# Cross-attention with residual and layer norm on one core: values' products ahead of the scores in full slots, loads ahead of slot 0, the last shifts on ScalarE

## The reference

```python
Q = (x @ w_q.T).reshape(B, S, 16, 32).transpose(0, 2, 1, 3)
K = (ctx @ w_k.T).reshape(B, -1, 16, 32).transpose(0, 2, 1, 3)
V = (ctx @ w_v.T).reshape(B, -1, 16, 32).transpose(0, 2, 1, 3)
attn = softmax(einsum('bhqd,bhkd->bhqk', Q, K) / sqrt(32))
c = einsum('bhqk,bhkd->bhqd', attn, V)     # back to (B, S, 512)
z = c @ w_o.T + b_o + x
out = (z - mean(z)) * rsqrt(var(z) + 1e-5) * gamma + beta
```

## Time and profile before

| what | us |
| --- | --- |
| median of 3 runs | 559.24 (558.02 to 559.49) |
| the profiled execution | 559.06 |
| its span, first to last instruction | 557.3 |
| PE busy | 533.4 (96%), 4522 products |
| DVE busy | 465.2 (83%) |
| POOL busy | 424.5 (76%) |
| ACT busy | 393.8 (71%) |
| mean granted TensorE clock | 0.992 |

### The profile page before, as it was taken

How to read it: one execution, slowest core, us unless ns; L and a number is a source line. 1 busy time by engine, 2 the same in 40 slices (tenths; PEclk the granted TensorE clock), 3 DMA queues, 4 the chain that set the end, 5 groups by cost and what they waited for, 6 DMA issues and landing times.

```text
span 557.3 us, 12699 instructions
## 1 busy us (share of the span) xinstructions
PE 533.4 (96%) x4522; PEld 365.2 (66%) x4522; DVE 465.2 (83%) x874; ACT 393.8 (71%) x733; POOL 424.5 (76%) x391
## 2 busy tenths in 40 slices
PE   8988889999999999999999999999999999998991
PEld 6755556766676666766676667666676667665561
DVE  7867658888888888988889888988888888988785
ACT  7636667777777777777777777777777777766662
POOL 1714778888888888888888888888888888776665
PEclk9999999999999999999999999999999999999996
DMA  8434552443344334442343334443343432322122
GB/s 303 150 86 132 147 162 70 131 129 95 95 130 131 102 91 125 130 123 84 113 133 109 120 95 125 107 123 100 120 121 98 133 103 84 85 67 72 44 76 95
DMA packets 74111, 63.23 MB, mean 113 GB/s; under 512 B 46528, under 2 KB 46528, under 8 KB 74048
## 3 DMA queue, kind: packets, MB, share of 16 engines
q1 hardware_dynamic: 74048, 62.42, 37.5%
HBM read 39.58 MB, written 16.78 MB: 101 GB/s over the span
## 4 chain that ended last, share of the span: by engine, by line
PE 81%; DVE 6%; DMA 4%; SPq 3%; issue 2%; POOL 2%; ACT 1%; DVEq 0%; POOLq 0%
PE ps_q L408 28%; PE ps_o L414 27%; PE ps_c L370 9%; PE ps_s L343 7%; DMA max_rows<-max_turned 4%; PE ps_s L353 3%; PE ps_q L281 2%; SPq L215 2%; PE ps_s L281 2%; PE ps_o L281 2%; DVE half_max L701 1%; DVE turned L696 1%; POOL y L877 1%; PE ps_c L288 1%; POOL y L875 1%
## 5 line engine op out<-in xcount | busy, mean ns | idle before, releaser
L408 PE MATMUL ps_q<-x_hi,wq_lo 64*128 64x512 f32 x448 | 186.8, 417 | 1.7 <-DVE values L666 1.6
L414 PE MATMUL ps_o<-wo_hi,c_lo 64*128 64x512 f32 x448 | 186.7, 417 | 0.0
L408 PE MATMUL ps_q<-x_hi,wq_hi 64*128 64x512 f32 x448 | 175.7, 392 | 0.0
L408 PE MATMUL ps_q<-x_lo,wq_hi 64*128 64x512 f32 x448 | 175.5, 392 | 0.0
L414 PE MATMUL ps_o<-wo_hi,c_hi 64*128 64x512 f32 x448 | 175.2, 391 | 0.0
L414 PE MATMUL ps_o<-wo_lo,c_hi 64*128 64x512 f32 x448 | 174.8, 390 | 0.0
L408 PEld LDWEIGHTS ps_q<-x_hi,wq_lo 64*128 64x128 f32 x448 | 82.4, 184 | 70.9 <-DVE z L745 45.3
L875 POOL TENSOR_TENSOR y<-y,gamma_row 128x512 f32<-128x512 f32 x60 | 77.6, 1294 | 58.9 <-ACT y L560 58.9
L847 POOL TENSOR_TENSOR x_lo<-xT_raw,x_hi 128x512 fp32r<-128x512 f32 x60 | 77.6, 1293 | 27.4 <-ACT x_hi L495 25.3
L853 POOL TENSOR_TENSOR c_lo<-c_raw,c_hi 128x512 fp32r<-128x512 f32 x64 | 82.7, 1292 | 17.3 <-ACT c_hi L495 17.2
L414 PEld LDWEIGHTS ps_o<-wo_hi,c_hi 64*128 64x128 f32 x448 | 82.6, 184 | 10.6
(11 more groups left out here) (104 smaller groups left out, 1114.5 us busy)
## 6 DMA issues: line engine op xcount, KB each, us to landing
xT_raw<-in_xT SPq DMA_DIRECT2D x64, 256.0 KB, 3.3
x_raw<-in_x SPq DMA_DIRECT2D x64, 256.0 KB, 2.9
out<-y SPq DMA_DIRECT2D x64, 256.0 KB, 2.4
max_rows<-max_turned SPq DMA_DIRECT2D x256, 16.0 KB
ctx_raw<-in_ctxT SPq DMA_DIRECT2D x4, 256.0 KB, 4.5
wk_raw<-in_wkT SPq DMA_DIRECT2D x4, 256.0 KB, 4.7
wq_raw<-in_wqT SPq DMA_DIRECT2D x4, 256.0 KB, 5.9
wv_raw<-in_wvT SPq DMA_DIRECT2D x4, 256.0 KB, 6.9
```

What stands on the lines that cost most here:

```text
L408: return nc.tensor.matmul(ps_q[:, 0, :], w[l][half, k, dims], x_[r][half, qc % 2, k, :], start=(half is lower and k == 0 and step == 0), s ...
L414: return nc.tensor.matmul(ps_o[:, 0, :], cx[l][half, k, tile], wo[r][half, k, :], start=(half is upper and k == 0 and step == 0), stop=(ha ...
```

## The change

- In the full slots `combine_values(t - 2)` comes ahead of `score(t)`.
- SP issues `wo_raw` (8 DMAs), the bias, gamma, beta and tiles 0 to 3 of `x_raw` ahead of its wait for the keys and of the first fill; slots 2 to 5 load one tile of `x_raw` each.
- In slots 1 to 3 `subtract_max(t - 1)` comes ahead of `project_values`. In slot 6 DVE makes `odd_values` ahead of `turn_max`.
- In slot 62 DVE makes `turn_max(61)` ahead of `divide(59)` and `statistics(54)`.
- The shifts of tiles 59, 60 and 61 are made by ScalarE as two operations on one column each: minus the mean, then times rstd.
- `WARM` is 8.
- `eps_column` (4 bytes in each partition) and the small statistics are allocated behind the streamed tensors.

```diff
@@
-    WARM = 10
+    WARM = 8
@@
-        eps_column = sb("eps_column", [P, 1], fp32)
 
         xT_raw = sb("xT_raw", [P, KT, CHUNK], fp32)
@@
+        half_max = sb("half_max", [P, 2, 32], fp32)
+
+        max_hl, max_turned = sb("max_hl", [P, 3, 32], fp32r), sb("max_turned", [P, 2, 32], fp32)
+        stats = sb("stats", [P, 8, 6], fp32)
+        mean_var = sb("mean_var", [P, 8, 2], fp32)
+        log_var, rstd, shift = (sb(n, [P, 8], fp32) for n in ("log_var", "rstd", "shift"))
+        eps_column = sb("eps_column", [P, 1], fp32)
@@ SP
-            sp.wait_ge(keys_zeroed, 2)
-            sp.wait_ge(keys_lo_done, G)
@@ SP
+            for k in range(KT):
+
+                for head in range(2):
+                    sp.dma_start(wo_raw[64 * head:64 * (head + 1), k, :],
+                                 woT_v[k, :, :].rearrange("(p h d) n -> h p d n", p=2, h=2)[head, :, :, :]
+                                 ).then_inc(wo_loaded[k], 16)
+            sp.dma_start(bias_row[:, :], b_o.partition_broadcast(P)).then_inc(bias_loaded, 16)
+            for row, src in ((gamma_row, gamma), (beta_row, beta)):
+                sp.dma_start(row[:, :], src.partition_broadcast(P)).then_inc(gains_loaded, 16)
+            for i in range(4):
+                load_x(i)
+            sp.wait_ge(keys_zeroed, 2)
+            sp.wait_ge(keys_lo_done, G)
             for t in range(OUT_LAG):
                 fill_max_rows(t)
                 load_ahead(t)
...
                 if 2 <= t <= 5:
-                    load_x(2 * t - 4)
-                    load_x(2 * t - 3)
...
+                    load_x(t + 2)
                 next_keys(t)
@@ PE, head
                 project_queries(t + 1)
+                if 1 <= t <= 3:
+                    subtract_max(t - 1)
...
-                if 1 <= t < OUT_LAG - 1:
+                if 3 < t < OUT_LAG - 1:
                     subtract_max(t - 1)
@@ PE, full slots
                 project_both(t + 1, t - OUT_LAG, True)
+                combine_values(t - 2)
                 score(t)
-                combine_values(t - 2)
@@ ACT
+            def shift_mean(i):
+                c = i % 8
+                nc.scalar.activation(shift[:, c:c + 1], mean_var[:, c, 0:1], ACT.Identity, scale=-1.0
+                                     ).then_inc(mean_negated_done, 1)
+                act.wait_ge(mean_negated_done, by_scalar(i) - by_scalar(59) + 1)
+                act.wait_ge(rstd_done, i + 1)
+                nc.scalar.activation(shift[:, c:c + 1], shift[:, c:c + 1], ACT.Identity, scale=rstd[:, c:c + 1]
+                                     ).then_inc(shift_done, 1)
@@ ACT, end
-            invert_deviation(59)
-            normalise(59)
...
+            for i in (59, 60, 61):
+                invert_deviation(i)
+                shift_mean(i)
+                normalise(i)
@@ DVE, head
+                if t == OUT_LAG - 1:
+
+                    odd_values(t // 2)
                 turn_max(t)
-                if t % 2 == 0:
+                if t % 2 == 0 and t < OUT_LAG - 1:
                     odd_values(t // 2)
@@ DVE, slot 62
+            turn_scores(61)
+            half_maxima(61)
+            fold_halves(61)
+            turn_max(61)
+            divide(59)
+            statistics(54)
+            add_residual(55)
+            queries_to_lo(63)
@@ POOL, end
             for i in (59, 60, 61):
-                shift_mean(i)
                 scale(i)
```

More of the change, by code:

```diff
@@ L78, in cross_attention_kernel @@
         turned = sb("turned", [P, 2 * CHUNK], fp32)
-        half_max = sb("half_max", [P, 2, 32], fp32)
-        max_hl, max_turned = sb("max_hl", [P, 3, 32], fp32r), sb("max_turned", [P, 2, 32], fp32)
         max_rows = sb("max_rows", [P, 2, CHUNK], fp32r)
@@ L89, in cross_attention_kernel @@
         x_raw = sb("x_raw", [P, 8, DM], fp32)
-        stats = sb("stats", [P, 8, 6], fp32)
-        mean_var = sb("mean_var", [P, 8, 2], fp32)
-        log_var, rstd, shift = (sb(n, [P, 8], fp32) for n in ("log_var", "rstd", "shift"))
         with ExitStack() as raw:
@@ L154, in cross_attention_kernel @@
         last_scaled_done, last_y_done = sem("last_scaled_done"), sem("last_y_done")
+        mean_negated_done = sem("mean_negated_done")
         def key_blocks(t, s, j):
@@ L242, in _ @@
                 load_ahead(t)
[L244 to L251, removed]
-                if 2 <= t <= 5:
-                    load_x(2 * t - 4)
-                    load_x(2 * t - 3)
-                if t == 5:
-                    for row, src in ((gamma_row, gamma), (beta_row, beta)):
-                        sp.dma_start(row[:, :], src.partition_broadcast(P)).then_inc(gains_loaded, 16)
+                if 2 <= t <= 5:
+                    load_x(t + 2)
                 next_keys(t)
@@ L772, in _ @@
                 queries_to_lo(t + 1)
+                if t == OUT_LAG - 1:
+                    odd_values(t // 2)
                 turn_max(t)
-                if t % 2 == 0:
+                if t % 2 == 0 and t < OUT_LAG - 1:
                     odd_values(t // 2)
-            for t in range(OUT_LAG, SLOTS - 1):
+            for t in range(OUT_LAG, SLOTS - 2):
                 i = t - OUT_LAG
```

## The result

| | us |
| --- | --- |
| before | 559.51 (558.02 to 560.62, 6 runs) |
| after | 573.05 (571.05 to 573.76, 6 runs) |
| ratio | 1.0236 [1.0214, 1.0259] |
| the profiled execution after, its span | 573.76, 571.8 |
| PE, DVE, ACT, POOL busy | 535.9, 470.7, 398.9, 423.8 |

A forecast was written before the change was run, and what follows sets the result against it. PE, with products back to back in the full slots, was taken to bound the kernel, leaving head and tail: head +16.0, full slots +2.1 and 0, tail -1.1 and -2.7, sum +14.3 on 559.06, giving 573.4 us; range 566 to 580.

The forecast's parts named there:

- First fill: Head: wo_raw's eight DMAs queue on two engines, 6.0 us a pair; subtract_max(0) waits until 51.4, +19.2 us.
- The lower end: Head, first fill: at 2.57 us per wo_raw DMA, the fill lands at 47.9 instead of 51.4.
- the share of 0.13: Head, sign of being right: DMA share near 0.13, two engines working, from some 24 to 46 us.
- Clock: Head: after 20 us idle PE returns at 1.2 GHz, 4 us at half speed, +2.0 us (0 to 4).
- rival (4): Head: clock stays full and wo_raw pairs run at 51 GB/s, 568 us; chance 0.12 together with (3).
- Rest of the head: From subtract_max(0) to the first full slot: fills land on time, 36.2 us instead of 41.4, -5.2 us.
- Full slots: The 56 full slots: 0.63 us less cover makes late fills of max_rows cost +2.1 us; PE's step changes by 0.
- Several new waits for `max_rows`: Full slots: listed among the signs that would show the forecast wrong; no size given.
- PE-neutral swap: Full slots: combine_values ahead of score keeps both PE transitions, 2.17 us against 2.16, taken as 0.
- Rivals (2) and (3): Full slots: (2) one more open load, 579 us, chance 0.10; (3) one transition saved, 567.8, 0.12 together with (4).
- Tail: Tail: earlier turn_max(61) brings PE's rows forward, -1.1 us; shifts on ScalarE bring z(63) forward, -2.7 us.
- Rival (1): Head: wo_raw's DMAs spread over other engines, early loads hidden, first fill at 31.6, 551.8 us; chance 0.09.

The follow-up runs named there:

- e1: The changed kernel with the eight wo_raw loads back behind the fills, in slots 1 to 4: 553.9 us, ratio 0.9891 against the kernel before.
- e2: The changed kernel with wo_raw still early but loaded by 16 DMAs of 32 partitions that use all engines: 560.1 us, ratio 1.0007 against the kernel before.
- e14: The changed kernel with 80 added products keeping PE busy ahead of subtract_max(0): 571.5 us, ratio 1.0202 against the kernel before.
- e3: The kernel before with only combine_values moved ahead of score in the full slots: 563.8 us against 559.8, ratio 1.0071.
- e11: e1 with the swap undone, score again ahead of combine_values: 551.4 us, ratio 0.9845 against the kernel before.
- e5: The kernel before with only turn_max(61) moved ahead of divide(59) and statistics(54): 558.7 us, ratio 0.9974.
- e13: As e2, with the bias moved to slot 1 and gamma and beta to slot 5: 556.2 us, ratio 0.9932 against the kernel before.
- e10: The changed kernel with only four of the eight wo_raw loads early, the others in slots 3 and 4: 565.4 us, ratio 1.0094 against the kernel before.
- e4: The kernel before with only the shifts of tiles 59 to 61 moved to ScalarE: 558.8 us, ratio 0.9971.
- e8: The kernel before with only eps_column and the small statistics allocated behind the streamed tensors: 558.7 us, ratio 0.9981.

## Why the prediction was right, step by step

The forecast of the total is better than its terms. Against the trace, the first fill is 2.1 us under the forecast, the rest of the head 1.1 over it and the tail 1.2 over it; that these nearly cancel is luck. What is shown is the mechanism of each term:

- **First fill, +19.2 forecast, +17.1 seen.** The mechanism was right: two engines, always the same, in order, 51 GB/s; e1 (the loads put back) removes the delay whole, e2 (more engines) two thirds of it. The mis-sized term is the pair of `wo_raw`, 6.0 us from the earlier trace rows: eight DMAs took 22.0 us from 21.9 on, 5.5 a pair. The pairs of before had fills and loads of `xT_raw` among them, of which I took off only 0.4. The lower end (2.57 each, 20.6) is what the first three steps show (2.5 to 2.6), until other loads ran beside them; with those it was too low by 1.4. The seven loads (4.6) and the fill (0.7) came as written. That bias, gamma and beta in a row move at 145 to 164 GB/s on all engines (e2, e1), and that the two engines are slower while loads run on the fourteen, I had not seen. For the same reason the share of 0.13, my sign for all of 24 to 46, held only until 32.
- **The Trainium skill's rule** ("DMA: Bandwidth & Descriptors", section "Why a DMA increments its semaphore by 16 and not by 1") spoke against the change, and e2 bears it out: with 32 as the slowest dimension the same bytes land by 28.0, with 2 by 43.8.
- **Clock, +2.0.** e14 gives 2.1. The granted clock was 0.50 from 34 on, in the wait, and until 54, some 5 us after PE began again. So rival (4), a clock that stays full, is out.
- **Rest of the head, -5.2 forecast.** -2.1 seen less 2.1 for the clock is -4.2. Of the missing 1.0, 0.2 is ahead of `score(3)` (e14's 8.94 at full clock, instead of 8.75) and 0.8 is slot 6: 7.33 us instead of 6.55. The fills did land on time: 4.0 to 4.5 us from `max_turned` to the rows in place in slots 1 to 6, where before they took up to 8.2. The combination waits 0.30 for c_raw of divide(3), and the first full slot 0.61 for `odd_values` (88.62 above). I had costed the moved `odd_values` at 0.15 of DVE time and not asked when it is asked for.
- **Full slots, +2.1 and 0.** In after the sum is exact, by two errors that cancel: the longer slots add 4.0 instead of 1.0 us, so +3.0 (forecast 2.1), and the step is 7.828 instead of 7.844, -0.9 (forecast 0). The wait is the one forecast: 0.5 us of cover are left of 1.2, and fills that land 0.6 to 2.0 us late now stop PE. But I took their number, three or four, from before. With the swap there are more: five to eight that take over 4.6 us in each of the eight traces with it, two to five in the six without, many of them 14 slots apart. In after, two of the five waits are for such new ones (fills 29 and 45). Why the swap makes more of them is open. Several new waits for `max_rows` also stood among my signs of being wrong; five came, and they are what this term is made of, so that sign was badly chosen. e3 and the e1/e11 pair give 4.0 and 2.6 for the whole swap, the tail included.
- **PE-neutral swap.** Right: 1.02, 0.34, 0.23, 0.23 as forecast, and the same plain slot in e3. Rivals (2) and (3), an open load more or a transition less for 5.6 us, are out: either would show as 0.1 us in the plain slot, and the largest difference, between e1 and e11, is 0.01.
- **Tail, -3.8 forecast, -2.6 seen.** The shifts gave their 2.7 at z(63), and finish(63) took 0.7 back beside POOL. I had written that POOL slows finish(62), and not that finish(63) comes under it once it is early. turn_max(61) moved PE's rows by 1.3 but the last product only by 0.6: the chain behind it, to `subtract_max(63)`, is late next (e5).
- **Rival (1)** (hidden loads) needed a landing before 37. e2 shows the turning point well: landing at 36.0, time equal to before.

## What to carry to other kernels

Before a load is put ahead of a small, urgent DMA in the same queue, read how many engines it uses and what a packet of it costs: what counts is not the bytes but the time of the busiest engine, here 22 us for 1 MB. A swap that is neutral on the bounding engine still spends somebody's cover; list the transfers whose cover it takes, and their slowest landings rather than the typical one, and allow for more slow ones than before. In a tail, ask of each operation that is brought forward what it will then run beside.

## What the runs showed of the hardware that was not expected

- Three broadcasts of a 2 KB row to 128 partitions, issued one behind the other, run slowly on all engines: 145 GB/s at a share of 0.96 (e2), 164 at 1.00 (e1), against 356 with plain loads in the same window (e13). One alone does not: packets of 84 ns for the most part (e13, slot 1). The cause is open.
- A 128 KB load on two engines takes 2.5 to 2.6 us while nothing else runs, and 2.65 to 4.1 beside loads on the other fourteen (after, e10).
- SP stood 12.60 us in issuing eight DMAs that lie on two engines, so the fill was issued 10.7 us late. Here that is hidden, since the two engines had work until 48.45.
- DVE's SCALAR_TENSOR_TENSOR of 128x512 takes 0.75 us alone and 1.43 to 1.71 while POOL works on a tensor of the same size (after, e4).
- The place of small tensors in SBUF alone moved the plain slot by 0.008 us of 7.84 (e8), together with the other edits by up to 0.02 (e11); the cause is open.
